# An adjacency unit laid over the partitions by segment first and row second

## The reference

```python
def reference(x, adj, weight, weight_u, weight_v, bias, proj_w, proj_b):
    h = jnp.maximum(_layernorm(x, axis=-1), 0.0)
    support = (h @ weight).reshape(-1, H, D).transpose(1, 0, 2)
    f1 = jnp.einsum('hnd,hd->hn', support, weight_u[..., 0])[:, None, :]
    f2 = jnp.einsum('hnd,hd->hn', support, weight_v[..., 0])[:, :, None]
    masked = leaky_relu(f1 + f2, 0.2) * adj
    mask = masked != 0
    e = jnp.where(mask, jnp.exp(masked - rowmax(masked)), 0)
    out = (e / e.sum(axis=2)) @ support          # per head
    return x + out + bias + h @ proj_w.T + proj_b
```

## Time and profile before

| | us |
|---|---|
| median of 3 runs | 1029.13 |
| lowest, highest | 1023.09, 1041.22 |
| the profiled execution, its own time | 1033.3 |
| its span, first to last instruction | 1031.5 |
| PE busy | 761.2 (74%) |
| DVE busy | 631.4 (61%) |
| POOL busy | 605.4 (59%) |
| ACT busy | 122.5 (12%) |

### The profile page before, as it was taken

How to read it: one execution, slowest core, us unless ns; L and a number is a source line. 1 busy time by engine, 2 the same in 40 slices (tenths; PEclk the granted TensorE clock), 3 DMA queues, 4 the chain that set the end, 5 groups by cost and what they waited for, 6 DMA issues and landing times.

```text
span 1031.5 us, 11116 instructions
## 1 busy us (share of the span) xinstructions
PE 761.2 (74%) x3013; PEld 458.3 (44%) x3013; DVE 631.4 (61%) x2507; ACT 122.5 (12%) x439; POOL 605.4 (59%) x732
## 2 busy tenths in 40 slices
PE   3898899998577776777776766778667776767754
PEld 1565555655144443534344434435344433434443
DVE  4555555564366666766666575666666666576763
ACT  1222222322010000001000000001010000000000
POOL 4444444444675847657585847557575857556661
PEclk9999999999668778788887767778887878767676
DMA  8999999999979898998989897989979898988610
GB/s 314 407 330 368 333 375 356 384 380 365 401 282 352 281 369 301 360 340 298 358 303 361 277 366 276 362 299 350 344 272 365 302 366 307 358 333 301 222 50 22
DMA packets 115390, 329.81 MB, mean 320 GB/s; under 512 B 13472, under 2 KB 40274, under 8 KB 115328
## 3 DMA queue, kind: packets, MB, share of 16 engines
q1 hardware_dynamic: 79232, 277.89, 72.1%
q0 software_dynamic: 18432, 34.30, 10.6%
q10 hardware_dynamic: 17664, 16.91, 5.0%
HBM read 328.99 MB, written 16.91 MB: 335 GB/s over the span
## 4 chain that ended last, share of the span: by engine, by line
PE 28%; DVE 21%; issue 15%; DMA 15%; another core or an unknown queue 9%; POOL 7%; ACT 2%; SPq 1%; ACTq 0%; POOLq 0%
PE ps_agg L440 11%; DMA att<-in_x 10%; PE ps_words L378 7%; DVE att L880 5%; DMA adj_raw<-in_adj 5%; POOL att L644 4%; PE ps_two L360 4%; PE ps_two L378 3%; DVE cand L733 2%; POOL out_tile L672 2%; DVE stats L767 2%; PE ps_agg L360 1%; DVE codes_rest L758 1%; PE ps_words L371 1%
## 5 line engine op out<-in xcount | busy, mean ns | idle before, releaser
L644 POOL DMA_INDIRECT att<-support_table,idx x384 | 394.5, 1027 | 265.0 <-DVE idx L792 139.9
L440 PE MATMUL ps_agg<-att,ident 128*128 128x260 f32 x640 | 209.8, 491 | 65.0 <-DVE att L880 43.5
L378 PE MATMUL ps_words<-adj_raw,pack_w 128*128 128x512 fp8e4 x640 | 195.6, 443 | 45.3 <-DMA adj_raw<-in_adj 41.6
L440 PEld LDWEIGHTS ps_agg<-att,ident 128*128 128x128 f32 x640 | 159.7, 254 | 117.4 <-issue 83.8
L378 PE MATMUL ps_two<-adj_raw,pack_w 128*128 128x512 fp8e4 x384 | 126.5, 476 | 55.3 <-DMA adj_raw<-in_adj 44.1
L378 PEld LDWEIGHTS ps_words<-adj_raw,pack_w 128*128 128x128 bf16 x640 | 61.8, 106 | 152.2 <-DMA adj_raw<-in_adj 60.8
L880 DVE TENSOR_TENSOR att<-att 128x1536 f32<-128x1536 f32 x64 | 114.9, 1835 | 0.6 <-ACT att L561 0.6
L733 DVE MAX8 cand<-ps_words 128x8 f32<-128x128 f32 x320 | 67.2, 283 | 74.0 <-PE ps_words L378 34.0
L378 PEld LDWEIGHTS ps_two<-adj_raw,pack_w 128*128 128x128 bf16 x384 | 38.1, 113 | 128.9 <-DMA adj_raw<-in_adj 62.3
L632 POOL COPY record<-att 128x8 f32<-128x8 f32 x64 | 14.4, 225 | 136.5 <-ACT att L513 136.5
L672 POOL TENSOR_TENSOR out_tile<-out_tile,base 128x256 f32<-128x256 f32 x64 | 72.2, 1150 | 12.7 <-DVE out_tile L892 12.7
(11 more groups left out here) (128 smaller groups left out, 817.1 us busy)
## 6 DMA issues: line engine op xcount, KB each, us to landing
adj_raw<-in_adj SPq DMA_DIRECT2D x256, 1024.0 KB
support_table<-att ACTq DMA_DIRECT2D x16, 520.0 KB, 7.3
att<-in_x SPq DMA_DIRECT2D x16, 512.0 KB, 8.0
out<-out_tile ACTq DMA_DIRECT2D x64, 128.0 KB
att<-support_table,idx POOLq DMA_INDIRECT x384
w_all<-in_proj_wT SPq DMA_DIRECT2D x2, 128.0 KB, 5.8
w_all<-in_weight SPq DMA_DIRECT2D x2, 128.0 KB, 6.2
uv_row<-in_weight_u SPq DMA_DIRECT2D x1, 128.0 KB, 3.7
```

Of the source, the lines that this page charges most:

```text
L378: mm = nc.tensor.matmul(ps_words[buffer_of(t)][:, k * 512:(k + 1) * 512], pack_w[:, u * UT + s, :], adj_low[:, u, s, k * 512:(k + 1) * 512 ...
L440: mm = nc.tensor.matmul(ps_agg[:, b, 0:ROW], ident[:] if k < OWN else onehotT[:, g % 2, b], gathered[:, g % RING, b, k], start=(k == 0), s ...
L644: pool.indirect_dma_start(gathered[:, g % RING, b, k, :], None, table, bass.IndirectOffsetOnAxis(idx[:, g % RING, b, k:k + 1], 0), bounds_ ...
```

## The change

The partitions of a step hold the segment first and the row second: partition m x 16 + n instead of n x 8 + m. A unit's two steps are loaded by one transfer each, of 512 KB, both counted on the unit's semaphore; PE waits for both. The pack constants follow: POOL makes `pack_at` by one iota, DVE masks it to the row number and compares it with 0 to get `pack_blk`; `pack_i` is shifted right by 4 instead of masked, to give the segment. POOL's two selects and its memset are gone, and DVE has two operations more.

```diff
-        adj_v = adj.rearrange("(T u s n) (m e) -> T u (n m) s e", u=UNITS, s=UT, n=ROWS_STEP, m=BITS)
+        adj_v = adj.rearrange("(T u s n) (m e) -> T u s m n e", u=UNITS, s=UT, n=ROWS_STEP, m=BITS)
...
-                    sp.dma_start(adj_raw[:, u], adj_v[t, u]).then_inc(s_adj_in[u], 16)
+                    for s in range(UT):
+                        sp.dma_start(adj_raw[:, u, s], adj_v[t, u, s]).then_inc(s_adj_in[u], 16)
...
-                pe.wait_ge(s_adj_in[u], 16 * (t + 1))
+                pe.wait_ge(s_adj_in[u], 16 * UT * (t + 1))
...
-            const(pool.memset(pack_blk[:], 1.0))
+            const(pool.iota(pack_at[:], [[-1, ROWS_STEP]], base=ROWS_STEP, channel_multiplier=1))
...
-            const(pool.affine_select(pack_blk[:], pack_blk[:], [[-BITS, ROWS_STEP]], ALU.is_ge, 0.0, base=0,
-                                     channel_multiplier=1))
...
-            const(pool.affine_select(pack_blk[:], pack_blk[:], [[BITS, ROWS_STEP]], ALU.is_ge, 0.0, base=BITS - 1,
-                                     channel_multiplier=-1))
...
-            n = step(v.tensor_single_scalar(pack_i[:], pack_i[:], BITS - 1, ALU.bitwise_and))
+            step(v.tensor_single_scalar(pack_at[:], pack_at[:], ROWS_STEP - 1, ALU.bitwise_and))
+            n = step(v.tensor_single_scalar(pack_i[:], pack_i[:], ROWS_STEP.bit_length() - 1, ALU.logical_shift_right))
...
+            step(v.tensor_single_scalar(pack_blk[:], pack_at[:], 0, ALU.is_equal))
```

More of the change, by code:

```diff
@@ L120, in gat_kernel @@
         pack_i = sb("pack_i", [P, 1], I32)
+        pack_at = sb("pack_at", [P, ROWS_STEP], I32)
         pack_blk = sb("pack_blk", [P, ROWS_STEP])
@@ L288, in gat_kernel @@
         table_rows = table[:, 0:HF].rearrange("(t p) d -> t p d", p=P)
-        POOL_CONSTS = 22
+        POOL_CONSTS = 20
         W_LOADS = 2 * KC + 4
@@ L698, in _ @@
             const(v.memset(seg_top[:], 0.0))
-            dve.wait_ge(s_pool_const, 14)
+            dve.wait_ge(s_pool_const, 12)
             dve.wait_ge(s_dve_const, 7)
             v.tensor_tensor(bit_mask[:], bit_one[:], bit_ramp[:], ALU.logical_shift_left)
-            n = step(v.tensor_single_scalar(pack_i[:], pack_i[:], BITS - 1, ALU.bitwise_and))
+            step(v.tensor_single_scalar(pack_at[:], pack_at[:], ROWS_STEP - 1, ALU.bitwise_and))
+            n = step(v.tensor_single_scalar(pack_i[:], pack_i[:], ROWS_STEP.bit_length() - 1, ALU.logical_shift_right))
             after(n)
```

## The result

The changed kernel takes 1638.72 us (median) against 1027.43 us for the kernel before, measured beside it: a ratio of 1.588, 95% interval 1.576 to 1.600. The forecast was 1,686 us, 2.9% above. The profiled execution took 1634.67 us with a span of 1632.9; that is the number to hold against 1,686.

The account below looks back on a forecast made before the run. Bound by transfers: on each of 8 loaded engines, 1,436.6 us adjacency plus 189.4 other traffic, with start and tail a span of 1,684.7, plus 1.8 outside it, gives 1,686 us. Range 1,530 to 2,750 us (0.79); own bounds 1,530 to 1,760.

Parts of the forecast that it names:

- What bounds the kernel: Whole kernel: transfers bind, engines busy 1.00 in the projection stage and 0.91 in the group stage, then a dependence-bound tail.
- The dealing out: Adjacency transfers: split by the outermost count of both sides, so 8 engines share each instead of 16.
- the upper end: Adjacency transfers: the bound taken, 8 engines and doubled time per engine, against a lower end of 16 engines at no cost.
- the forecast's case: Adjacency on 8 engines with packets as now: 1,686 us, own range 1,530 to 1,760, chance 0.50.
- rival 2: Adjacency writes: engines sharing an SBUF port clash and packets lengthen; 3,123 us if all double, 2,405 at 1.5 x; chance 0.35.
- The diagnostic of the prediction: Packet count on queue q1 after the change: 79,232 means 8 shares per adjacency transfer, 83,328 means 16.
- Constants, PE's waits, SP's issues at nothing: Startup constants, PE's unit waits and 512 adjacency issues by SP (188 us, at most 510): claimed to add no time.
- PE hidden at a lower clock: Tiles on PE: even at 1.2 GHz 16.8 us each, hidden behind a tile's transfer of 22.4 us.
- The sum: One loaded engine: 1,436.6 us adjacency plus 189.4 other traffic, together 1,626; with start and tail a span of 1,684.7 us.
- The tail: After the last adjacency words: 61.5 us bound by dependences, less 8 us of traffic already counted.
- Rival 1: Adjacency transfers: split follows the destination's 128 partitions, all 16 engines still share, nothing happens; 1,035 us, chance 0.10.
- Rival 3: Adjacency transfers: eight engines with load eased elsewhere, or a split into more than 8; 1,060 to 1,530 us, chance 0.05.

Follow-up runs that it names:

- no_rows: The changed kernel with every gather index put out of the table's bounds, so gathers complete but move no rows; 1542.24 us, ratio 1.595 to the kernel before.
- row_first_halves: The kernel before with one edit, each adjacency unit loaded in two transfers of 512 KB, row first as before; 949.01 us, ratio 0.994.
- row_first_eight: As row_first_halves, but the source written as 8 groups of 16 neighbouring 4 KB runs, each group starting 60 KB after the last; 1622.1 us, ratio 1.697.
- by_segment: The changed kernel with each unit in 8 transfers of 128 KB, one per segment, 16 rows outermost; one execution, 1704.28 us.
- rates: No layer computed: SP alone streams adjacency into a ring of four 1 MiB slots, one access pattern per stage; 405, 208, 104 GB/s for outermost counts 128, 8, 4.
- row_first_8: Stage of rates: 512 KB transfers to 128 partitions, source in 8 overlapping groups of 16 neighbouring 4 KB runs; 208 GB/s.
- after_again: The changed kernel, unaltered, run once more in the second lot on another chip; 1624.32 us, ratio 1.695 to the kernel before.
- segment_first: Stage of rates with the changed kernel's own adjacency pattern, 8 segments outermost and 16 rows 32 KB apart, streamed alone; 128 GB/s.

## Why the prediction was right, and where it was off

**What bounds the kernel** was right: the transfers. Taking the gathers' bytes away (no_rows) gave back nearly the time that their packets take on an engine, and matmuls of 628 ns instead of 387 left the loaded engines as full as the sum below shows them; no run held PE's clock up to price that by itself.

**The dealing out** was the step on which all hung, and the trace of before could not decide it. row_first_halves and row_first_eight decide it: as many bytes, the same destination, as many transfers and runs of 4 KB, an outermost source count of 128 or of 8, 949 or 1,622 us. In the prediction this step was a choice of the upper end, with 0.85 on it by the chances of the forecast's case and rival 2; it was not read off a trace. The rule of the Trainium skill, "DMA: Bandwidth & Descriptors", section "Why a DMA increments its semaphore by 16 and not by 1" (the largest number up to 16 that divides both sides' slowest counts), agrees with every pattern run here: shares of 1.02, 0.51 and 0.26 for 128, 8 and 4. The diagnostic of the prediction, 79,232 or 83,328 packets, read right both times.

**Constants, PE's waits, SP's issues at nothing**: right. SP's issues became much longer than I read off, 1,215 ns at the median and up to 6,231 instead of 368 and 996; my upper end of 510 us for all of them was exceeded (512 x 1.2 = 622 us). In the chain SPq L310 has 7%, and 13% in by_segment. They don't set the rate of a loaded engine: in rates the stage row_first_8 ran at 208 GB/s with issues of a like length:

```profile
L48 SPq DMA_DIRECT2D buf<-in_adj x96: 598/1793/2453, 673.7 to 900.0; - x96
```

**PE hidden at a lower clock**: right, though the clock fell only to 0.62 in the group stage.

**The sum** was 52 us too long (1,686.5 against 1,634.7), and the term that failed is the first step of it, that the packets' recorded times on one engine add up to time. By the rows of after a loaded engine has 744.6 x 268.4 / 277.9 x 2 = 1,438 us of adjacency, 25.4 of q1's rest, 120.8 of gathers (7.4%), 50.6 on q10 and 3.3 of instructions, 1,638 us in all, some 4% more than the 1,574 us between the two ends. (That deals q1's time by bytes. The packet records give the 4 KB packets 703.8 us in the mean of 16, and a sum of 1,623 us, 3% more.) So recorded packets overlap, if all but the adjacency is dealt evenly to 16 engines; rates shows the overlap directly, a share of 1.02 for one queue alone. Scaling the sum of 1,626 us by 0.96 gives 1,561, with the ends 1,620 and as a time 1,622; most of the 13 us that this is short are the gathers, whose packets took 120.8 us instead of 109.3. The tail holds, 61.5 us before and 58 now with the same 0.13 of traffic.

That q1's packets kept their time to 0.1% is in part luck. It compares with the first timing, in which the 4 KB packets of the kernel before took 174.0 ns in the mean (171.8 after the change). In the later lots row_first_halves, with 16 engines, has 167.1 ns and 718.4 us of q1 per engine, after_again 170.9 ns and 740.4 us (45.7% of 1620.1): against that they grew by 3%. The same sum with row_first_halves' rows (q1 75.8%, gathers 10.9%, q10 5.5% of 947.8 us) gives a span of some 1,629 us for the 1,620 of after_again; there the growth of the packets and their overlap nearly cancel.

**Rival 1** (nothing happens) is out by the packet count. **Rival 2** (engines hinder each other) got 0.35. In the profiled executions of the full kernel it is absent as a steady effect: 23.7 GB/s per loaded engine, not 16.0, and a median packet of 159 ns as before. Clashes now and then may be part of what lies between 23.7 and 26.0: 7% of the packets are longer than 220 ns, 2% in row_first_halves. But its mechanism exists: 120 to 128 GB/s in the streams that run in step, and by_segment, where sixteen engines do no better than eight. Its price at full effect, an estimate from these streams: 268.4 MB at 128 GB/s are some 2,100 us for the adjacency alone, with gathers, x and ends near 2,350 us; at 120 GB/s 2,240 and near 2,490. That is not the 3,123 I gave it, because the mean packet grew by 1.6 to 1.75 and not by 2. One execution of the changed kernel, the 2,414 us at the top, has a time between these two figures; whether it ran in step no trace can tell, so rival 2 is excluded for the profiled executions only. **Rival 3** did not occur.

## What to carry to other kernels

The order in which a transfer's source is walked is part of its speed: put a count that 16 divides outermost on both sides, keep the engines' shares of the destination apart (by_segment has 16 engines and is no faster than eight), and look at the completion packets (queue packets less data runs, divided by transfers) to see how many engines share it. A DMA line at five tenths with an engine waiting for the transfers need not be spare bandwidth: here it was half the engines idle. A change of layout that looks free, since it keeps bytes, run length and partitions, should be tried as its two parts (here the halving and the outermost count) before it is believed.

## What the runs showed of the hardware that was not expected

- Engines that write the same part of SBUF share its rate: 56 GB/s for 8 engines on partitions 0 to 7, 141 for 16 engines on 16 neighbours at a time, at least 182 for 8 engines with 4 partitions each, and 208 where 8 engines have 16 each and are out of step. The Trainium skill, "SBUF — State Buffer", section "Door 1: The DMA port swizzle", has partitions 0 to 7 on two ports of 27.2 GB/s, which makes an estimate of 54 GB/s: the run agrees within 3%. The 141 lie above the 109 that the same table gives for 16 neighbours, four ports; no run here explains that (transfers to several sets of 16 were under way at a time).
- Streams of eight engines that started in step stayed in step for 390 us at 128 GB/s, and eight packets of offset lift the same pattern to 207. In the full kernel the offset is worth nothing.
- The kernel before ran 7% slower at its first timing than in both later lots, the changed one 1%. The traces put the difference in the group stage: 329 GB/s at a share of 0.91 before (260 to 970 us), 370 at 0.98 in row_first_halves of the first lot (240 to 890 us), with 367 and 370 in the projection stage. The kernel before has no trace in the later lots, and the cause is open.
- An issue of an 8-share transfer takes SP at least 598 ns where a 16-share one of the same 512 KB takes 326 at least, and it grew to microseconds where an eight-share stream had transfers under way (2,677 ns at the median in segment_first, 1,793 in row_first_8), which did not keep row_first_8 from 208 GB/s. What such an issue waits for, no run shows.
